# Causal attention: the sums of a unit move behind the scores of the next unit

## The reference

```
xn = layernorm(x, g1)
q = xn @ Wq.T
kv = xn @ Wkv.T
k, v = (kv[..., :DIM_HEAD], kv[..., DIM_HEAD:])
q, k = (l2norm(q), l2norm(k))
sim = jnp.einsum('bhid,bjd->bhij', q, k)
sim = jnp.where(causal_mask, max_neg, sim)
attn = jax.nn.softmax(sim)
out = jnp.einsum('bhij,bjd->bhid', attn, v)
out = out @ Wout.T
return layernorm(out, g2)
```

## Time and profile before

| what | value |
|---|---|
| median of 3 runs | 3413.22 us (3405.32 to 3420.39) |
| the profiled execution's own time | 3414.89 us |
| its span, first to last instruction | 3413.2 us |
| granted TensorE clock over the span | 0.958 |
| TensorE busy over the span | 90% |
| ScalarE busy over the span | 59% |
| causal phase, first to last store issued | 1799.5 to 2630.9 us |

### The profile page before, as it was taken

The page is one execution under the profiler, slowest core; times in us unless marked ns, Lnnn a source line. Parts: engine busy times, 40 slices in busy tenths (PEclk is TensorE's granted clock), DMA queues, the critical chain, the costliest instruction groups (busy, mean ns, idle before and its releaser), DMA issues. The chain is left out here.

```text
span 3413.2 us, 44434 instructions
## 1 busy us (share of the span) xinstructions
PE 3083.3 (90%) x12374; PEld 1648.1 (48%) x12374; DVE 1745.2 (51%) x2671; ACT 2022.3 (59%) x4072; POOL 1064.4 (31%) x890
## 2 busy tenths in 40 slices
PE   5888888799999999967679999999998879999998
PEld 2333333477777777722234444444443634444443
DVE  5999999455555555579933333333342521111111
ACT  5777776266666666546657777777775523333333
POOL 4788788122222222223323333333332100000000
PEclk8999999799999999988889999999998979999999
DMA  3545444000000000011100000000000300000000
GB/s 99 170 146 166 155 156 149 32 15 22 17 22 17 22 17 22 14 45 49 48 18 14 14 16 17 14 14 14 14 14 31 138 34 19 18 18 28 18 18 13
DMA packets 104264, 159.17 MB, mean 47 GB/s; under 512 B 11904, under 2 KB 44560, under 8 KB 104208
## 3 DMA queue, kind: packets, MB, share of 16 engines
q1 hardware_dynamic: 97872, 144.89, 12.6%
q10 hardware_dynamic: 6336, 13.60, 1.3%
HBM read 85.77 MB, written 4.72 MB: 27 GB/s over the span
## 5 line engine op out<-in xcount | busy, mean ns | idle before, releaser
L1354 POOL TENSOR_TENSOR d_pr<-d_pr,d_keep 128x512 f32<-128x512 f32 x256 | 320.1, 1271 | 565.4 <-ACT d_pr L1512 565.4
L770 POOL TENSOR_TENSOR b_pn<-b_e,b_inv 128x616 f32<-128x616 f32 x128 | 161.3, 1260 | 605.4 <-DVE b_inv L951 605.4
L256 POOL TENSOR_TENSOR a_bx<-a_bcopy,a_drive_u 128x512 f32<-128x512 f32 x256 | 319.7, 1269 | 18.0 <-DVE a_state L523 10.4
L523 DVE TENSOR_TENSOR_SCAN a_state<-a_decay,a_bx 128x512 f32<-128x512 f32 x256 | 311.1, 1215 | 5.5 <-POOL a_bx L256 5.3
L276 PE MATMUL a_py<-a_prod,consts 128*128 128x512 f32 x512 | 284.9, 639 | 2.8 <-DVE a_t L503 1.5
L1921 PE MATMUL f_ph<-f_hb,wb 128*128 128x512 f32 x512 | 231.2, 595 | 6.3 <-ACT f_hb L1954 6.3
L1921 PE MATMUL f_ph<-f_ha,wb 128*128 128x512 f32 x512 | 229.0, 596 | 2.3 <-DVE f_ha L1983 2.3
L454 ACT ACTIVATE a_decay<-a_delta,neg_a 128x508 f32<-128x508 f32 x256 | 174.5, 682 | 73.4 <-DVE a_state L523 73.1
L926 DVE TENSOR_REDUCE b_peak<-b_pscore 128x8 f32<-128x616 f32 x128 | 102.3, 799 | 216.5 <-PE b_pscore L807 216.5
L876 ACT ACTIVATE b_yy<-b_py,y_bias 128x154 f32<-128x154 f32 x512 | 169.1, 382 | 67.8 <-PE b_py L816 67.7
L1576 DVE TENSOR_SCALAR d_ln<-d_pn 128x512 f32<-128x512 f32 (+1 forms) x160 | 101.8, 636 | 196.3 <-PE d_pn L1407 196.3
(11 more groups left out here) (281 smaller groups left out, 6390.6 us busy)
## 6 DMA issues: line engine op xcount, KB each, us to landing
a_bcopy<-rows SPq DMA_DIRECT2D x256, 256.0 KB, 3.5
wb<-in_wb ACTq DMA_DIRECT2D x14, 480.0 KB, 4.2
a_xf<-in_x SPq DMA_DIRECT2D x16, 256.0 KB, 4.1
a_xt<-in_x ACTq DMA_DIRECT2D x16, 256.0 KB, 3.6
x<-a_xo SPq DMA_DIRECT2D x16, 256.0 KB, 2.3
b_xf<-x SPq DMA_DIRECT2D x32, 128.0 KB, 2.0
b_xt<-x SPq DMA_DIRECT2D x32, 128.0 KB, 2.0
x<-b_xo SPq DMA_DIRECT2D x32, 128.0 KB, 2.0
```

The costliest lines, as they stand in the source:

```text
L256: gp.tensor_tensor(bx[:, k % 4, :], bcopy[:, k % 4, :], drive_u[:, p, :], ALU.mult).then_inc(*bxt.step("bx"))
L523: V.tensor_tensor_scan(state[:, j % 2, :], decay[j % 2][:], bx[:, j % 4, :], 0.0, ALU.mult, ALU.add).then_inc(*vs.step("scan"))
L770: gp.tensor_tensor(heads(pn[:, j % 2, :]), heads(e[:, j % 2, :]), over(inv[:, j % 2, :], CTX), ALU.mult).then_inc(*pnt.step("n"))
L1354: gp.tensor_tensor(half, half, keep[:].unsqueeze(1).to_broadcast([128, QP, SEQ]), ALU.mult).then_inc(*gmt.step(f"m{odd}"))
```

## The change

`summed` says in which slot the sums of a unit stand, on TensorE, ScalarE and VectorE alike. Before, unit 0, 1 and 2 stand in slots 3, 5 and 7 and unit 3 in slot 1 of the next step. After, they stand in slots 2, 4 and 6 and in slot 0 of the next step. In these slots the code places `weighted` right behind `scores` on TensorE, the denominators' L1519 and L1521 right behind the exponentials on ScalarE, and the product L1582 behind the maximum on VectorE. In slot 4 the roots of piece 0, the keys', stood behind the exponentials on ScalarE; they now stand first, as in the other slots. Nothing is added or removed, no transfer and nothing on GpSimd moves.

```diff
         def summed(g, p, k, main, tail):
-            if k % 2 == 0:
+            if k % 2:
                 return None
-            if k == 1:
+            if k == 0:
                 return (g - 1, 1 - p, UNITS - 1, UNITS * g - 1) if tail else None
-            return (g, p, (k - 3) // 2, UNITS * g + (k - 3) // 2) if main else None
+            return (g, p, (k - 2) // 2, UNITS * g + (k - 2) // 2) if main else None
...
                     for k in range(SLOTS):
-                        if k != 4:
-                            if u := piece(UNIT, g, p, k, front, main):
-                                roots(*u)
+                        if u := piece(UNIT, g, p, k, front, main):
+                            roots(*u)
                         if u := piece(LENGTH, g, p, k, front, main):
                             squares(*u)
...
                             A(den[:], den[:], ACT.Exp, scale=-1.0).then_inc(*sdt.step("inv"))
-                        if k == 4:
-                            if u := piece(UNIT, g, p, k, front, main):
-                                roots(*u)
```

## The result

The changed kernel takes 3588.27 us (median of 4 runs, 3582.42 to 3590.45) against 3412.01 us before: 1.0508 times, 95% interval 1.0492 to 1.0525. The profiled execution's span is 3586.9 us against 3413.2, 173.7 us more. The forecast was 3603 us, the range 3548 to 3640.

The account below looks back on a forecast made before the run. TensorE's queue was taken as the bound. Four chains losing cover, less one pause, gave +4.80 us a group, 147 us in all; clock falls added 41: 3415 + 147 + 41 = 3603 us, range 3548 to 3640.

Parts of the forecast that it names:

- the four chains: Work running from TensorE over ScalarE and VectorE and back; each loses the 1.86 us of sums as cover in every group.
- C: L1460 to the next scores, slots 6, 7, 0: the 3.70 us stretch can't shrink, +1.86 us a group.
- D: Lengths of piece 3 to the output half in slot 1: 4.32 us shrinks to 3.79, +1.33 us a group.
- B: L1452 to L1456 on TensorE: 3.36 us shrinks to 2.88, +1.38 us a group.
- A: Lengths of piece 4 to lengths of piece 0: 5.47 us shrinks to 4.34, +0.73 us a group.
- allowance of 0.15 us for the semaphore: Time from the end of an awaited operation to TensorE's start, read from product to scores and counted in chains.
- two pauses that both had a fall: TensorE pauses of 2.06 us (filling stage) and 2.17 us in the kernel before, with granted clock 0.59 and 0.52 behind them.
- hold up the squares: Slot 4: keys' roots ahead of the squares could cost up to 1.4 us without the 1.86 us of sums as cover.
- the pause of 0.50 us: TensorE's wait ahead of the lengths of piece 2, forecast to go as the sums fill it: -0.50 us a group.

Follow-up runs that it names:

- the run with work in the pause: The changed kernel with the projection of piece 3 in slot 7 made three times instead of once: 3552.49 us.
- unit 2 alone: The kernel before with only the sums of unit 2 moved from slot 7 to slot 6: 3518.22 us, 1.0318.
- the change without its second edit: The changed kernel with the keys' roots kept behind the exponentials and the denominators' roots in slot 4: 3628.11 us, 1.0632.
- unit 1 alone: The kernel before with only the sums of unit 1 moved from slot 5 to slot 4, keys' roots unmoved: 3512.16 us, 1.0298.

## Why the prediction was right

**The bound and the cover.** Right: the four chains lost their cover, at the four places named, and nothing else waits. One group without a fall takes 31.95 us (mean of the two kinds, 31.9 and 32.0, and of the run with work in the pause), forecast 32.2.

**The terms.** The chains were put up to 0.2 us too long: C 3.70 against 3.60 (and, in alternate groups, 3.70), D 3.79 against 3.69, B 2.88 against 2.68, A 4.34 against 4.25. The allowance of 0.15 us for the semaphore was too much: in the changed kernel TensorE starts 0.05 to 0.06 us behind the end of the record that it waits for, at all four places (the copy ends at 2248.77, the lengths start at 2248.83). That is the whole error of A and D and half of B's; the other half lies between the tail's root on ScalarE and VectorE's next operation, 0.96 us (L1523 to L1584 in the changed kernel) instead of 1.06 (L1527 to L1588). In part it was made good by something left out: the first matmuls behind a pause take longer to the next (L1456 to the scores 0.63 us, 2256.89 to 2257.52, against 0.52 before; the output 1.92, 2239.73 to 2241.65, against 1.82). From the distances the four give 1.76 + 1.23 + 1.18 + 0.64 - 0.50 = 4.31 us; the groups grew by 4.59. Of the 0.28 between them 0.21 are these slower starts, and 0.05 the alternate groups of C.

**The clock.** Right in kind: in the changed kernel the pause of chain C, and it alone, brings the falls; filling it took all of them away. Five falls in six groups were forecast, 41 us; there are 21 in the phase, about five in seven, 36 us. No row gave that share, it was set by two pauses that both had a fall, so that it came near is in part luck. The price of one was right: 1.65 us forecast, 4.57 - 2.93 = 1.64 measured. The granted clock, forecast as 0.93 to 0.96, is 0.96 from 1860 to 2600 us. The Trainium skill ("TensorE: Matmul & The Clock Gate", Why this matters for your kernels) warns only of longer pauses; by it the clock would have stayed up, which it did in about one group of four. Here the measurement decides: a pause of 2.2 us is long enough to be priced.

**The sum.** 147 us for the chains and 41 for the clock were forecast, 188. Of the 168.2 us between the stores 36 are the clock's, so 132 the chains'. The rest of the span's 173.7 us lies outside of these stores: the filling of the phase and its end, and the other phases. So the forecast of 3603, 14 us above the profiled execution's 3588.66, had 15 us too much for the chains and 5 too much for the clock, and lacked these 5.5.

**The second edit.** Here the prediction's time was right and its account wanting. It asked only whether the edit would hold up the squares, found 1.86 us of sums to hide that, and took nothing. It didn't ask what would become of the keys behind the denominators' roots if the edit were left out: there the edit is worth 40 us. And the pause of 0.50 us, which the prediction credited to the sums' new place, goes with this edit alone (3400.31 us). It also goes without the edit when the sums move (the runs with unit 2 alone and with the change without its second edit have no such wait), so only one of the two was needed.

**Left open.** Why the clock falls behind the pair of 1.18 and 1.01 us 16 times in the run with unit 1 alone, and only twice in the run without the second edit, which has the same pair in each group. There 20 of the 22 falls lie behind the pause ahead of the scores, and two, at 2213 and 2558 us, behind the pair (granted clock 0.58 from 2557.50 to 2560.50 us). The pauses are alike, what TensorE did in the microseconds around them differs. No run tells these apart. Nor does any run tell why some pauses of 2.15 and 2.24 us have a fall behind them and others of the same length have none.

## What to carry to other kernels

In an engine's fixed order a block of independent work is worth most between the two ends of a chain over other engines. Before moving it, list for each stretch that it leaves the chain's length and what work remains there; the difference is the loss, whatever the total of work. When two edits come together, price each against the other's presence as well as against the kernel before: here one edit is faster alone and mends 40 us of what the other spoils.

## What the runs showed of the hardware

The clock of TensorE fell behind 21 pauses of 2.15 to 2.24 us in some 29 groups, behind two of about 1.7 us, and never behind single ones of 1.2 to 1.3 us; a fall made 4.57 us of 2.93. Not expected: 1.9 us of useless matmuls per group made the kernel 36 us faster, and two pauses of 1.18 and 1.01 us with 1.13 us of matmuls between them brought the clock down as well, 16 times in one kernel and twice in another.
